# Attention-and-FFN layer on one core: unit sums, stats store and late outputs in another order

## What is computed

```python
x = L0_attn_x                                  # (8, 512, 512) f32: 8 chunks of 512 tokens
xn = layernorm(x)
q, k, v = xn @ Wq.T + bq, xn @ Wk.T + bk, xn @ Wv.T + bv
kv_sum = cumsum((elu(k) + 1) * v, axis=1)
s = ((elu(q) + 1) * kv_sum) * SCALE @ Wo.T + bo
h = fwht(xn * SU_ug) / 64
h = silu(h @ W_gate.T * (Wscale_ug[2048:] * 64)) * (h @ W_up.T * (Wscale_ug[:2048] * 64))
h = fwht(h * SU_dp) / 64
g = silu(h @ W_down.T * (Wscale_dp * 64))       # W_down: (512, 2048)
out = x + s * g
```

## Time and profile before

| what | value |
|---|---|
| median of 3 runs | 1316.68 us (1313.84 to 1318.09) |
| the profiled execution | 1323.87 us, of it 1322.1 us span |
| PE busy | 1267.6 us, 96% |
| DVE, ACT, POOL busy | 957.7, 616.8, 86.0 us |
| DMA | 220.96 MB, mean 167 GB/s |

### The profile page before, as it was taken

One profiled execution on the slowest core, in us unless ns is written; L12 is line 12 of the kernel. 1 busy time (PEld: TensorE's weight loads), 2 busy tenths in 40 slices (PEclk: granted clock), 3 DMA queues, 4 the chain that ended last, 5 costly groups with the idle time before them and its releaser, 6 DMA issues.

```text
span 1322.1 us, 16183 instructions
## 1 busy us (share of the span) xinstructions
PE 1267.6 (96%) x5896; PEld 572.3 (43%) x5896; DVE 957.7 (72%) x1444; ACT 616.8 (47%) x910; POOL 86.0 (7%) x137
## 2 busy tenths in 40 slices
PE   5998999999999999999998899999999899999997
PEld 3543444444344444444443344444444344444443
DVE  6999999877656777767574768776773867775714
ACT  5894656431235555551324555544233555554212
POOL 1001001211000000100113101000000000000000
PEclk9999999999899999999999899999999999999999
DMA  9533553677754466644537424233634332332431
GB/s 374 206 127 120 202 201 146 224 279 250 218 225 147 144 216 240 206 177 132 219 132 281 150 105 159 100 124 94 201 141 146 127 128 98 126 128 72 128 121 70
DMA packets 66847, 220.96 MB, mean 167 GB/s; under 512 B 13136, under 2 KB 19024, under 8 KB 52048
## 3 DMA queue, kind: packets, MB, share of 16 engines
q1 hardware_dynamic: 51536, 177.98, 37.9%
q0 software_dynamic: 9648, 31.99, 7.2%
q10 hardware_dynamic: 5584, 9.96, 2.2%
HBM read 166.40 MB, written 53.50 MB: 166 GB/s over the span
## 4 chain that ended last, share of the span: by engine, by line
PE 52%; DVE 5%; DMA 3%; issue 3%; ACT 2%; POOL 1%; SPq 0%; DVEq 0%; ACTq 0%
PE bank L2307 39%; PE bank L2373 6%; PE bank L2398 3%; PE bank L2493 3%; DMA scr_m<-mean_root 1%; ACT work L1168 1%; ACT work L1171 1%; DVE work L1588 1%; DMA ring<-scr_s 1%; DVE work L1572 1%; DVE h_all L1946 1%; DMA h_all<-scr_df 0%; POOL h_all L899 0%; DMA h_all<-scr_f 0%; DVE work L1578 0%
## 5 line engine op out<-in xcount | busy, mean ns | idle before, releaser
L2307 PE MATMUL bank<-xops,ring 128*128 128x512 f16 x2772 | 608.5, 381 | 19.3 <-DVE work L1588 7.1
L2307 PEld LDWEIGHTS bank<-xops,ring 128*128 128x128 f16 x2772 | 270.6, 98 | 356.2 <-issue 20.1
L2187 PE MATMUL bank<-xops,ring 128*128 128x512 f16 x1008 | 225.1, 379 | 1.3 <-DVE ring L1744 1.3
L1151 ACT ACTIVATE work<-bank 128x512 f32<-128x512 f32 x198 | 117.8, 595 | 222.0 <-PE bank L2307 207.5
L1572 DVE TENSOR_TENSOR work<-bank,work 128x512 f32<-128x512 f32 x198 | 133.6, 687 | 112.0 <-PE bank L2307 101.4
L2493 PE MATMUL bank<-h_all,ring 128*128 128x512 f16 x768 | 169.9, 384 | 4.5 <-DMA ring<-scr_d 4.3
L2187 PEld LDWEIGHTS bank<-xops,ring 128*128 128x128 f16 x1008 | 97.9, 98 | 124.8 <-issue 8.9
L2493 PEld LDWEIGHTS bank<-h_all,ring 128*128 128x128 f16 x768 | 75.7, 99 | 98.0 <-DMA ring<-scr_d 5.3
L1198 ACT ACTIVATE h_all<-work 128x512 f16<-128x512 f32 x116 | 70.5, 624 | 60.8 <-DVE work L1615 59.0
L1624 DVE TENSOR_TENSOR h_all<-work,h_all 128x512 f16<-128x512 f32 x116 | 79.4, 688 | 7.8 <-ACT h_all L1198 6.6
L1578 DVE SCALAR_TENSOR_TENSOR work<-work 128x512 f32<-128x512 f32 x64 | 44.0, 690 | 52.3 <-ACT work L1171 52.0
(11 more groups left out here) (273 smaller groups left out, 1321.2 us busy)
## 6 DMA issues: line engine op xcount, KB each, us to landing
ring<-scr_g SPq DMA_DIRECT2D x72, 1024.0 KB, 4.8
ring<-scr_d SPq DMA_DIRECT2D x16, 1024.0 KB, 6.5
scr_g<-ring SPq DMA_DIRECT2D x22, 512.0 KB, 3.3
h_all<-in_ug_t SPq DMA_DIRECT2D x8, 1024.0 KB, 12.1
ring<-in_down_t SPq DMA_DIRECT2D x6, 1024.0 KB, 6.7
scr_g<-ring POOLq DMA_DIRECT2D x12, 512.0 KB, 5.3
work<-in_x_t SPq DMA_DIRECT2D x6, 1024.0 KB, 7.4
scr_g<-h_all POOLq DMA_DIRECT2D x12, 512.0 KB, 3.7
```

The lines of the kernel that those rows point to most:

```text
L1151: act.activation(tile(g, j), chain_bank(g)[:, :], ACT.Copy).then_inc(copied, 1)
L2187: mm = pe.matmul(plain_bank(g, j)[:, :], at[:, s, 2 * dh + kk, r, :], xops[:, kk, xs, PLAIN_B[dh][c], :], start=(n == 0), stop=(n == len(t ...
L2307: mm = pe.matmul(to[:, :], weight_of(slot, s, b, kk), at, start=(a == 0 and m in (P1, P2, P5)), stop=(a == 5), skip_group_check=True)
```

## The change

Four things are changed.

1. Unit sums. down_high stores the folded weight in another layout, scr_u, by four DMAs in place of one, so that a unit is loaded by one DMA of 512 KB. That load is issued from ACT's queue, no longer POOL's. All six units now stand in pair 1. x_sums is parted in x_adds and x_low; x_adds, x_low and x_high of the next pair's first half, t_high, and units 0 and 1 are put between the adds and copies of pair 1's O groups.
2. Stats. DVE transposes mean_root in 32x32 blocks into mean_root_t (one more instruction), and SP stores it by four DMAs of 16 rows of 128 bytes. The store is parted from the spread: for pair 1 a quad load stands between them, for pairs 2 and 3 load_x.
3. Outputs. Pair 2's outputs 4 and 5 stand in groups 0 and 1 of pair 3, outputs 6 and 7 in group 4. SP stores six of them behind the fourth load and the last two behind the eighth.
4. x_high's wait for PE in pair 2 is now for the last product of group 21 of the pair before, as it was already in pair 3.

```diff
+LATE_OUTS = {0: (4,), 1: (5,), 4: (6, 7)}
...
+            def store_stats(p):
+                sp.wait_ge(mean_root_made, p)
+                for b in range(KB):
+                    sp.dma_start(scr_m[:, 32 * b:32 * b + 32], mean_root_t[32 * b:32 * b + 4 * TB, :]) \
+                        .then_inc(mean_root_stored, 16)
+
             def spread_stats(p):
 
-                sp.wait_ge(mean_root_made, p)
-                sp.dma_start(scr_m.rearrange("m t p -> p m t"), mean_root[:, :, :], allow_slow_non_contiguous=True) \
-                    .then_inc(mean_root_stored, 16)
-                sp.wait_ge(mean_root_stored, 16 * p)
+                sp.wait_ge(mean_root_stored, 64 * p)
...
             for n in range(KB, 2 * KB - 1):
                 load_first_quad(n)
                 if n == KB:
+                    store_stats(1)
+                elif n == KB + 1:
                     spread_stats(1)
...
-                            store_pair(p - 1)
+                            store_pair(p - 1, range(6))
+                    if p > SEVEN_FROM and n == 7:
+                        store_pair(p - 1, (6, 7))
                     if n == GROUPS + (4 if p < SEVEN_FROM else 3) and p < PAIRS - 1:
+                        store_stats(p + 1)
                         load_x(p + 1)
                         spread_stats(p + 1)
...
-                act.dma_start(scr_df[e, :, :].rearrange("p (r k n) -> p r k n", r=KB, k=KB), fly_down) \
-                    .then_inc(df_stored, 16)
+                for j in range(KB):
+                    half, q0 = j // 2, 2 * (j % 2)
+                    to = scr_u[2 * q0 + e % 2:2 * q0 + 4:2, :, e // 2, half, :].rearrange("q p n -> p q n")
+                    act.dma_start(to, fly_down[:, j, :, :].rearrange("p (q k) n -> p q (k n)", q=2)).then_inc(df_stored, 16)
...
+            def load_unit(u):
+
+                if u < 2:
+                    act.wait_ge(quad_done, 3 * KB)
+                    act.wait_ge(df_stored, 64 * KB)
+                else:
+                    act.wait_ge(unit_summed, u - 1)
+                act.dma_start(unit_part(u, 0).bitcast(F32), scr_u[u, :, :, :, :].rearrange("p r h n -> p r (h n)")) \
+                    .then_inc(unit_loaded[u % 2], 16)
...
-                if p > SEVEN_FROM and g < 2:
-                    pair_outputs(p - 1, (4 + 2 * g, 5 + 2 * g))
-                if p == SEVEN_FROM and g < UNITS - 4:
-                    unit_add(4 + g)
-                    unit_low(3 + g)
-                    if g == UNITS - 5:
-                        unit_low(4 + g)
+                if p > SEVEN_FROM and g in LATE_OUTS:
+                    pair_outputs(p - 1, LATE_OUTS[g])
...
-                dve.tensor_scalar(mean_root[:, 0, :], mean_var[:, :, 0], 1.0, None, ALU.mult)
-                prep.after(dve.tensor_scalar(mean_root[:, 1, :], rstd[:, :], X_SCALE, None, ALU.mult))
-                dve.sem_inc(mean_root_made, 1)
+                dve.tensor_scalar(mean_root[:, 0:2 * TB], mean_var[:, :, 0], 1.0, None, ALU.mult)
+                prep.after(dve.tensor_scalar(mean_root[:, 2 * TB:4 * TB], rstd[:, :], X_SCALE, None, ALU.mult))
+                dve.transpose(mean_root_t[:, :], mean_root[:, :]).then_inc(mean_root_made, 1)
```

More of the change, by code:

```diff
@@ L849, in _ @@
                     load_pair_res(p)
-            store_pair(PAIRS - 1)
+            store_pair(PAIRS - 1, range(8))
             for t in range(TB):
@@ L1319, in o_groups @@
                 g = GROUPS
-                for n in range(3):
-                    copy_sum(p, g, n)
+                copy_sum(p, g, 0)
+                if p < SEVEN_FROM:
+                    x_high(p + 1, 0)
+                copy_sum(p, g, 1)
+                copy_sum(p, g, 2)
                 copy_sum(p, g + 1, 0)
                 take(p, g, C21)
+                if p < SEVEN_FROM:
+                    t_high(p + 1, 0)
                 copy_sum(p, g + 1, 1)
+                if p < SEVEN_FROM:
+                    unit_high(0)
+                    load_unit(2)
                 copy_sum(p, g + 1, 2)
+                if p < SEVEN_FROM:
+                    unit_high(1)
+                    load_unit(3)
                 take(p, g + 1, C21)
@@ L1394, in _ @@
                 silu_outs(2 * p)
+                load_unit(0)
+                load_unit(1)
                 o_groups(p)
-                x_high(p + 1, 0)
-                t_high(p + 1, 0)
-                unit_high(0)
                 x_high(p + 1, 1)
-                unit_high(1)
+                unit_high(2)
+                load_unit(4)
                 t_high(p + 1, 1)
-                unit_high(2)
                 unit_high(3)
+                load_unit(5)
+                unit_high(4)
+                unit_high(5)
                 silu_outs(2 * p + 1)
@@ L1534, in x_sums, with x_adds @@
             def x_sums(p, kk):
-                n = 2 * p + kk - 2
+                x_adds(p, kk)
+                x_low(p, kk)
+            def x_adds(p, kk):
                 b11, b21, b12, b22 = (x_ln[:, k, :] for k in (kk, 2 + kk, KB + kk, KB + 2 + kk))
@@ L2161, in _ @@
                     continue
-                for g in (GROUPS, GROUPS + 1):
-                    for j in (C11, C22, C12):
-                        add(p, g, j)
-                outputs(2 * p)
-                x_sums(p + 1, 0)
-                t_low(p + 1, 0)
-                unit_add(0)
-                x_sums(p + 1, 1)
-                unit_add(1)
-                unit_low(0)
-                t_low(p + 1, 1)
+                g = GROUPS
+                add(p, g, C11)
+                x_adds(p + 1, 0)
+                add(p, g, C22)
+                x_low(p + 1, 0)
+                unit_add(0)
+                add(p, g, C12)
+                add(p, g + 1, C11)
+                unit_add(1)
+                add(p, g + 1, C22)
+                unit_low(0)
+                add(p, g + 1, C12)
+                t_low(p + 1, 0)
+                outputs(2 * p)
                 unit_add(2)
                 unit_low(1)
+                x_sums(p + 1, 1)
                 unit_add(3)
                 unit_low(2)
+                t_low(p + 1, 1)
+                unit_add(4)
+                unit_low(3)
+                unit_add(5)
+                unit_low(4)
+                unit_low(5)
                 outputs(2 * p + 1)
```

54 lines of the change are left out of this document (19 added, 35 removed).

## The result

| kernel | median us | lowest to highest | runs | profiled execution, its span |
|---|---|---|---|---|
| before | 1317.05 | 1313.84 to 1320.32 | 8 | 1323.87, 1322.1 |
| changed | 1309.40 | 1307.01 to 1312.75 | 8 | 1309.14, 1307.2 |

The ratio is 0.9945 (95% interval 0.9928 to 0.9961): the change gains 7.2 us, 5.1 to 9.5 by the interval. The forecast was 19.4 us and 1297.3, with a range from 1292 to 1306. The time is outside it. The direction was right and the size too large by 12 us. Between the two profiled executions the span fell by 14.9 us, twice what the medians show.

What follows compares the result with a forecast made beforehand. TensorE, busy 1267.6 of 1322.1 us, was taken as the bound, gains coming from its idle or half-clock time. 14.0 + 6.0 + 2.0 - 1.2 - 1.4 = 19.4 us off the median 1316.68 gave 1297.3, range 1292 to 1306.

Steps and rivals of the forecast that it cites:

- Border 1 to 2: Start of pair 2: units leave groups 0 and 1, so the stretch falls from 52.90 to 38.92 us, gaining 14.0.
- The chained times of the last unit_low and the first silu: Before pair 2's chunk 3: last unit_low near 693 and first silu near 696, about 9 us of room.
- Rival 3: Unit chain ends late, so first waits at pair 2's start return; half of 14.0 would give 1304.3 us; chance 0.10.
- Border 0 to 1: Before pair 1: stats store no longer blocks the down-weight load; 3.02 us wait and 3.0 of slow clock go, 6.0.
- Rival 1: Load waits belong to the profiled execution, timed runs never had them; 8.0 us of gain go, 1305.3 us; chance 0.15.
- Pair 2's down projection: Load for P5 issued some 14 us sooner, ahead of the stats' blocking; PE's whole 2.02 us wait goes.
- O groups: Pair 1: x_high(2, 0) on ACT between copies of P1 and P6 makes PE idle 1.2 us anew.
- Outputs: Pair 3: group 1 waits 1.54 us, group 4 waits 2.86 and loses 1.55 of clock; costs 1.4 us.
- one for one in a V group: Pair 3's outputs: work added to DVE in a V group returns in full as PE wait, above a bare 0.20 us.
- Rival 2: Pair 3's group 4 hides its outputs, DVE being ahead by then; gain 23.9 us, 1292.8 us; chance 0.15.
- The clock term: Pair 3: PE's clock halved behind group 4's 2.86 us wait, costing 1.55 us, but not behind group 1's 1.54.
- The rest: Down_high's extra stores in pair 0, 0.37 us per issue, and unit loads moved to ACT's queue: nothing, taken as covered.

Runs made afterwards that it cites:

- stats_only: The kernel before with only the new block store of the stats and its new place; 1316.66 us, ratio 0.9996.
- before_again: The kernel before, unchanged, timed and profiled a second time; 1317.65 us, ratio 0.9994.
- after_again: The changed kernel, unchanged, timed and profiled a second time; 1309.32 us, ratio 0.9937 to the kernel before.
- load_behind: The changed kernel with ACT's late loads of the weight sums moved behind one more copy, transfers unchanged; 1309.30 us, ratio 0.9951 to the kernel before.
- units_only: The changed kernel without the stats' block store and with the outputs where they were, x_high's wait kept; 1306.87 us, ratio 0.9919 to the kernel before.

## Why the prediction was off, step by step

The forecast gain was 19.4 us; measured were 7.2, 8.3 and 5.9 in three groups. By terms:

- **Border 1 to 2, +14.0.** Right: 14.00 by the first two profiles, 13.8 by the second two (52.69 and 38.92). The chained times of the last unit_low and the first silu were within 3 us. Rival 3 did not come.
- **Border 0 to 1, +6.0.** Wrong in the median. This is the step that failed most: with the down projection's term it makes the 8.0 us forecast for the stats, of which stats_only shows 0.5 (at most 1.8). The prediction took the wait of 3.02 us and the clock behind it for a property of the kernel, with the words that a load issued 6.3 us before its use "should be late in any run". It was so late in one profile of six, because of another load that took 8.5 us instead of 5.2. The text had seen that 7.2 us of the profiled execution were missing from the median and that no row showed where. It then took the whole sum off the median all the same. Rival 1 held the answer to this term, with a chance of 0.15; its own time of 1305.3 us is still 4 us too low, for the terms below.
- **Pair 2's down projection, +2.0.** The mechanism was right, the size half: 0.8 us on average in the other five profiles (1.0 in all six), less two waits of 0.35 us that come with the block store and were not forecast.
- **O groups, -1.2.** 0.82 to 0.84 us of wait; the stretch from the quads of chunk 2 to pair 2 is 1.05 longer (95.19 and 96.24 us). Right.
- **Outputs, -1.4.** 1.3 us by waits (-1.34 + 2.65) and some 2 us in the median (the intervals overlap). The rule "one for one in a V group" held to 0.02 us in both groups. Rival 2 (group 4 hides them) is out. The clock term is less sure than it was written: behind waits of 2.85 or 2.86 us it fell in two of three profiles of the changed kernel, and where it fell it cost 1.69 us, not 1.55.
- **The rest, nothing.** Wrong: it held the long issue, 1.7 us. Down_high's added instructions were priced where they stand, at 0.37 us each; they took 0.50 (1.5 us more a quadrant), and it is right that PE does not wait for them there. Their effect came 260 us later, through the place of the next fetch of ACT's program.

With the terms as measured, 14.0 + 0 + (1.0 - 0.7) - 1.0 - 1.3 - 1.7 = 10.3 us. Between the spans of before_again (1317.8) and after_again (1306.2) lie 11.6 us; between their medians 8.3. The remaining 2 to 3 us of the median (8.3 in that group, 7.1 on average) I can't place; their cause stays open. Both kernels have small waits of pair 1 that come and go from one execution to the next, and single profiles don't show their mean.

## What to carry to other kernels

A wait for a DMA in one profiled execution is a sample: where the profiled time lies above all the timed ones, part of the excess can lie in just such waits (here 4.98 of 7.2 us ahead of pair 1), and a second profile, or a run with that part alone, has to come before their gain is taken off the median. Work that is added to an engine should go to the group in which that engine has slack, and the same four outputs cost nothing that the trace shows in groups 0 and 3, and some 5 to 7 us more in the median in the other two places tried. After adding instructions to an engine, look for idle time of kind "issue" far behind the edit, and for a packet of kind "instruction" in it.

## What the runs showed of the hardware

- Twelve instructions more on ACT, DMA issues or tiny copies, made one transfer issue 260 us later take 3.6 to 4.9 us instead of 0.43. A packet of kind "instruction" lies inside it in all ten cases, and behind the issues in all eight others. It comes when ACT has begun 708 rows, with the twelve instructions and without (710 in load_behind), so it goes with ACT's program. That the fetch holds ACT up is the likeliest reading. The same packet leaves no mark in the eight others, where ACT waits 2.2 to 2.6 us for PE at that place; the other fetches were not looked at one by one.
- TensorE's clock behind one and the same wait is not fixed. Behind 2.86 us, 66 matmuls took 16.09 us in before_again (a mean granted clock of 0.59 from 1036 to 1040, so for a part at its 1.2 GHz level) and 14.40 in units_only and after_again, where the clock stayed at 1.00 (2.4 GHz). Of the 13 profiles with a wait of 2.85 or 2.86 us in pair 3 it fell in nine. For after_again, the stretch behind the wait:

```profile
1054.00:1058.00 4.00, 4.00 (x21) 1.00 0.41 158
```

- Two profiles of the kernel before differ by 4.3 us of span (1322.1 and 1317.8). Pair 1 starts 4.98 us later in the first; most of that is the wait of 3.02 us and the clock behind it, which go back to one load that took 3.3 us longer.
